# An xLSTM block with a look-up FFN on one core: two phases instead of one, the look-up spread over later blocks

## The reference

```
out = x + attn(xn) + ffn(xn)

attn(x): h = rmsnorm(x) * norm1
         q, k = h @ wq, h @ wk (8 heads of 32);  v, o = h @ wv, h @ w_og (8 heads of 64)
         i, f = 15 * tanh((h @ w_ig + b) / 15), 15 * tanh((h @ w_fg + b) / 15)
         F = cumsum(log_sigmoid(f));  D[s,t] = F[s] - F[t] + i[t], causal;  m = rowmax(D)
         C = (q @ k.T / sqrt(32)) * exp(D - m);  n = max(|rowsum(C)|, exp(-m))
         hh = rmsnorm_per_head((C / n) @ v) * mh_w * sigmoid(o)
         x1 = x + hh @ w_out
         return x1 + (silu(h2 @ w_gate) * (h2 @ w_up)) @ w_down,  h2 = rmsnorm(x1) * norm2   # 2048 wide

ffn(x):  gate, up, down = lut[gate_idx], lut[up_idx], lut[down_idx]    # 16 values, 1376 wide
         return (silu(x @ gate.T) * (x @ up.T)) @ down.T
```

## Time and profile before

| | |
|---|---|
| runs | 2776.36, 2777.57, 2778.02 us; median 2777.57 |
| profiled execution | 2779.31 us, its span 2777.5 us, mean granted clock 0.953 |
| TensorE, DVE, ScalarE, GpSimd busy | 2493.6, 1295.4, 809.4, 598.7 us |
| DMA | 431.78 MB, 155 GB/s over the span |

### The profile page before, as it was taken

The page is one execution under the profiler, slowest core; times in us unless marked ns, Lnnn a source line. Parts: engine busy times, 40 slices in busy tenths (PEclk is TensorE's granted clock), DMA queues, the critical chain, the costliest instruction groups (busy, mean ns, idle before and its releaser), DMA issues.

```text
span 2777.5 us, 32515 instructions
## 1 busy us (share of the span) xinstructions
PE 2493.6 (90%) x11024; PEld 2000.8 (72%) x11024; DVE 1295.4 (47%) x2240; ACT 809.4 (29%) x1474; POOL 598.7 (22%) x497
## 2 busy tenths in 40 slices
PE   4545877677999999999999999999999999999988
PEld 3324656566777788778877788778877888778877
DVE  6886874776134632364125622364235523463221
ACT  4653535552114211321123211321123211321111
POOL 1332540322111211131112211121112211121111
PEclk8757999889999999999999999999999999999999
DMA  5213765335542354244542355135533455135544
GB/s 198 72 46 122 283 235 197 129 122 224 193 173 92 137 189 182 83 141 167 200 153 91 129 197 197 72 134 188 184 128 107 152 189 196 62 138 188 194 182 154
DMA packets 95754, 431.78 MB, mean 155 GB/s; under 512 B 10496, under 2 KB 10496, under 8 KB 65664
## 3 DMA queue, kind: packets, MB, share of 16 engines
q1 hardware_dynamic: 80400, 393.56, 39.3%
q10 hardware_dynamic: 10464, 19.14, 2.1%
q0 software_dynamic: 4752, 17.30, 1.6%
HBM read 371.77 MB, written 58.20 MB: 155 GB/s over the span
## 4 chain that ended last, share of the span: by engine, by line
issue 52%; PE 16%; POOL 9%; ACT 3%; DVE 2%; DMA 2%; POOLq 0%; ACTq 0%; DVEq 0%; SPq 0%
POOL hidden_lo L1757 5%; PE acc L549 4%; PE up_bank L549 3%; PE gate_bank L549 3%; PE bank_b L549 3%; PE bank_a L549 2%; ACT look_w L924 1%; POOL MX L1770 1%; POOL vw L1785 1%; DMA gu<-gu_parts 1%; POOL rh L1702 1%; POOL rs L1702 1%; DMA first_rows<-xn 1%; DVE look_w L1281 0%; PE gate_bank L583 0%
## 5 line engine op out<-in xcount | busy, mean ns | idle before, releaser
L1757 POOL TENSOR_TENSOR hidden_lo<-hm,hidden_hi 128x512 fp32r<-128x512 f32 x216 | 279.6, 1294 | 1504.8 <-ACT hidden_hi L866 1504.7
L549 PE MATMUL acc<-dn,hidden_hi 128*128 128x512 f32 x1728 | 548.0, 399 | 24.6 <-POOL hidden_lo L1757 24.6
L1325 DVE SCALAR_TENSOR_TENSOR th<-th,gate_bank 128x512 f32<-128x512 f32 x216 | 147.8, 684 | 642.6 <-ACT th L861 642.6
L549 PEld LDWEIGHTS acc<-dn,hidden_hi 128*128 128x128 f32 x1728 | 324.0, 191 | 93.1 <-issue 20.2
L866 ACT ACTIVATE hidden_hi<-hm 128x512 fp32r<-128x512 f32 x216 | 135.9, 629 | 848.0 <-PE acc L549 824.2
L549 PE MATMUL gate_bank<-hT_hi,gu 128*128 128x512 f32 x1024 | 340.9, 394 | 30.4 <-DVE hT_lo L1547 19.4
L549 PE MATMUL up_bank<-hT_hi,gu 128*128 128x512 f32 x1024 | 339.7, 393 | 0.7 <-DVE hm L1331 0.6
L549 PE MATMUL acc<-dn,hidden_lo 128*128 128x512 f32 x864 | 339.6, 393 | 0.0
L861 ACT ACTIVATE th<-gate_bank 128x512 f32<-128x512 f32 x216 | 128.8, 596 | 471.8 <-PE gate_bank L549 471.8
L1331 DVE SCALAR_TENSOR_TENSOR hm<-th,up_bank 128x512 f32<-128x512 f32 x216 | 148.0, 685 | 241.6 <-PE up_bank L549 241.0
L549 PE MATMUL up_bank<-xT_hi,gu 128*128 128x512 f32 x704 | 256.8, 426 | 0.0
(11 more groups left out here) (233 smaller groups left out, 3711.3 us busy)
## 6 DMA issues: line engine op xcount, KB each, us to landing
gu<-gu_parts SPq DMA_DIRECT2D x200, 1024.0 KB, 4.8
dn<-dn_parts SPq DMA_DIRECT2D x200, 512.0 KB, 3.4
gu_parts<-gu SPq DMA_DIRECT2D x16, 1024.0 KB, 6.3
gu_parts<-look_w POOLq DMA_DIRECT2D x17, 512.0 KB, 3.1
ix<-idx ACTq DMA_DIRECT2D x33, 256.0 KB, 2.7
raw_gu<-w_gu SPq DMA_DIRECT2D x16, 512.0 KB, 6.9
qkT<-x SPq DMA_DIRECT2D x8, 1024.0 KB, 6.1
xn<-x SPq DMA_DIRECT2D x8, 1024.0 KB, 7.9
```

Source lines behind the costliest of these rows:

```text
L549: mm = pe.matmul(dst, l[a], r[c], start=first and k == 0 and n == 0, stop=last and k == len(lhs) - 1 and n == 2)
L1325: dve.scalar_tensor_tensor(th[:], th[:], 1.0, GB[:], ALU.add, ALU.mult).then_inc(vec_gate.sem, 1)
L1757: pool.tensor_tensor(HH[1][:], hm[:], HH[0][:].bitcast(f32), ALU.subtract).then_inc(pool_hid.sem, 1)
```

## The change

The work is put in another order, in two phases.

- Block 0: front, then units alone. Beside them the MLP weights of tiles 0 to 10 are split (`mlp_hi_`, `mlp_lo_`: gate, up and now also down on ScalarE and GpSimd) and stored; tiles 11 to 15 follow in block 1's front.
- MLP phase. For blocks 1 to 7: front, then 16 MLP tiles of the block before (`tiles(at)`, `mb = previous(at)`) with this block's units, out projection and h2 between tiles 0 to 10. x of the next block is normed at tiles 11 to 13. At the end the sums are copied to `XN[half]` and stored by SyncE as `mlp_rows`; x1 is stored as `x1_rows` at tile 11. Then 16 MLP tiles of block 7 without units (`TAIL`).
- Look-up: blocks 2 to 7 only, 11 chunks of gate, up or down per batch item, 5 in its first half and 6 in the second. DVE takes its steps by `TAKEN`: 6 or 8 at tile 8, and 11 or 13 at each of tiles 11 to 14. ScalarE takes at tile t those levels that the steps of tile t - 1 allow; levels of the first chunk at tile 0. Stores are now SyncE's. The buffers lie over the v and o weights, 4 MB, which SyncE loads again at the end of each of these blocks (`reload_vo`), behind the last chunks' stores.
- Ghost phase: for each block, 11 ghost tiles and nothing else of TensorE but the transposes of x, which is loaded, normed and transposed a second time. x, x1 and the MLP's rows are loaded (`rest`, 3 MB) and added at tile 3. SyncE stores the rows when the last sum is made.

The diff, cut to its core:

```diff
-NCH = 3 * NF
-PHASES = [0, 4, 21, 24, NCH]
+NCH = NF
+CHUNKS = [(0, 5), (5, NF)]
+TAKEN = [[0] * 8 + [6, 0, 0, 11, 11, 11, 11, 0], [0] * 8 + [8, 0, 0, 13, 13, 13, 13, 0]]
...
+# SyncE, one block of the MLP phase
+            def tiles(at):
+                b, half = at
+                mb = previous(at)
+                for t in range(NM):
+                    if t + 1 < NM:
+                        load_gu(MLP, mb, t + 1)
...
+                    else:
+                        load_gu(MLP, at, 0)
+                    load_dn(MLP, mb, t)
...
+                    if looks(at):
+                        ready = steps_taken(half, t - 1) // STEPS_V if t else 0
+                        for n in range(CHUNKS[half][0] + stored, ready):
+                            store_chunk(at, n)
+                            stored += 1
+                        if t == NM - 1:
+                            for n in range(*CHUNKS[half]):
+                                if n >= CHUNKS[half][1] - 2:
+                                    pair_stored(sp, at, n)
+                            reload_vo(1)
+                            reload_vo(2)
+                wait(sp, vec_out, mb, NB - 1)
+                first = (b * HALVES + half) * TOK + -TOK
+                sp.dma_start(rows_of(mlp_rows, first), XN[half][:]).then_inc(st_mlp[half], 16)
...
+# SyncE, the ghost phase
+                    for t in range(NF):
+                        if t + 1 < NF:
+                            load_gu(GHO, at, t + 1)
+                        else:
+                            load_gu(GHO, (b, half + 1), 0)
+                        load_dn(GHO, at, t)
+                        if t == 0:
+                            wait(sp, pe_xT, (b, half - 2), NB - 1)
+                            load_next(at)
+                            first = (b * HALVES + half) * TOK + -BATCH * SEQ
+                            sp.wait_ge(st_out[half], b * 16 + (16 - BATCH * 16))
+                            sp.dma_start(rest[half], rows_of(x, first)).then_inc(ld_rest[0], 16)
+                            sp.wait_ge(vec_rest.sem, vec_rest.before(at))
+                            sp.dma_start(rest[2], rows_of(x1_rows, first)).then_inc(ld_rest[1], 16)
+                            sp.dma_start(rest[3], rows_of(mlp_rows, first)).then_inc(ld_rest[2], 16)
+                    wait(sp, vec_out, at, NB - 1)
+                    sp.dma_start(rows_of(out, first), rest[half]).then_inc(st_out[half], 16)
...
+# ScalarE, tile t of the MLP phase, behind hid(t - 1) and tanh(t)
+                    if looks(at):
+                        ready = steps_of_levels(at[1], steps_taken(at[1], t - 1) if t else 0)
+                        look_up(at, min(ready, looked + 13) if t < NM - 2 else CHUNKS[at[1]][1] * STEPS_A)
+                        if t == NM - 2:
+                            upper(at, CHUNKS[at[1]][1] - 1)
...
+# DVE, tile t, behind gated(t) and product(t)
+                    if looks(at):
+                        look_up(at, steps_taken(half, t))
+                    if t == 11:
+                        ln_stats(at, XN[1 - half], 1 - half, b * 16 + (16 + 16 * half))
...
+                    for i in range(NB):
+                        x_T(at, i)
+                wait(dve, MLP.down, mb, NM - 1)
...
+                for i in range(NB):
+                    dve.tensor_copy(XN[half][:, i, :], ACC[i][:]).then_inc(vec_out.sem, 1)
...
+# TensorE, the ghost phase
+                    for t in range(NF):
+                        gate(GHO, at, t, act)
+                        up(GHO, at, t, act)
+                        if t >= NF - NB:
+                            x_T(at, t - NF + NB, XN[1 - half], ghosts=True)
+                        if t:
+                            down(GHO, at, t - 1, NF - 1)
+                    down(GHO, at, NF - 1, NF - 1)
```

More of the change, by code:

```diff
@@ L32, with steps_taken, steps_of_levels @@
 READ_BY = {upper: 3 + s for s, (lower, upper, bit) in enumerate(MUX)}
[L35 to L68, removed]
+TAKEN = [[0] * 8 + [6, 0, 0, 11, 11, 11, 11, 0], [0] * 8 + [8, 0, 0, 13, 13, 13, 13, 0]]
+def steps_taken(half, t):
+    return CHUNKS[half][0] * STEPS_V + sum(TAKEN[half][:t + 1])
+def steps_of_levels(half, j):
+    first, end = CHUNKS[half]
+    a = first * STEPS_A
     while a < end * STEPS_A:
         n, q = divmod(a, STEPS_A)
-        if q == 7:
+        if n == first:
+            need = 0
+        elif q == 7:
             need = n * STEPS_V
         elif q == 0:
-            need = n * STEPS_V if n in PHASES else (n - 1) * STEPS_V + 3
+            need = (n - 1) * STEPS_V + 3
         else:
@@ new lines, in up, with down @@
+            def up(of, at, t, act, stage=None):
+                z = slot(of, at, t)
+                if t == 0 and stage:
+                    wait(pe, vec_rows, stage, 0, "factors")
+                else:
+                    wait(pe, of.hm, at, t - 1)
+                split(UB[:], [(WGU[:, z, 1, 0, toks(k)], WGU[:, z, 1, 1, toks(k)]) for k in range(KT)],
+                      [pair(act, S_, k, S_) for k in range(KT)]).then_inc(of.up.sem, 1)
+            def down(of, at, t, last):
+                z = slot(of, at, t)
+                if t == 0:
+                    pe.wait_ge(vec_out.sem, vec_out.before(at))
+                pe.wait_ge(ld_dn[z], loads(of, at, t))
+                wait(pe, of.low, at, t, "lo")
@@ L838, in _ @@
-            for t in range(NF):
-                gate(LAST, t, t % 2, XT, loads(LAST, t))
-                up(LAST, t, t % 2, XT)
-                if t:
-                    if t == 1:
-                        pe.wait_ge(vec_out.sem, vec_out.before(LAST))
-                    down(LAST, t - 1, (t - 1) % 2, loads(LAST, t - 1), first=t == 1)
-            down(LAST, NF - 1, (NF - 1) % 2, loads(LAST, NF - 1), last=True)
+                    front((b, half))
+                    tiles((b, half))
+            tiles(TAIL)
@@ L1333, in front @@
             def front(at):
                 b, half = at
-                first, second = here(at, FIRST), here(at, SECOND) and PHASES[2] < NCH
+                first = here(at, FIRST)
                 R1 = r1[half]
```

1172 lines of the change are left out of this document (518 added, 654 removed).

## The result

The changed kernel takes **2904.05 us** (median of four runs, 2903.31 to 2906.26) against 2777.41 us before: a ratio of 1.046, 95% interval 1.044 to 1.048. The forecast was 2887 us, slower, with a range of 2750 to 2955. The profiled execution has a span of 2901.5 us.

A forecast was written before the change was run, and what follows sets the result against it. TensorE's order of work was taken to bound the kernel from block 2 on, look-up on DVE and ScalarE before. 2618 + 155 look-up + 100 ghost loads + 5 fronts + 9 tiles without units = 2887 us, range 2750 to 2955.

The forecast's parts named there:

- Start: Block 1's front was to begin at 192 us and its first gate tile at 245 us (220 to 275).
- 8.8 us a round: In block 0, each of eleven rounds of units beside an MLP tile's weight split takes 8.8 us, ending at 172 us.
- 13 beyond 40: Block 1's front: 40 us of groups and products, 53 with five splits, the last store and first stored-tile load.
- The bare blocks: A block without its 11 ghost tiles takes 217 us; block 1 needs 177 after its front's 40.
- Look-up: In blocks 2 to 7, look-up beside tiles adds 155 us in all, 4.7 us a chunk.
- ScalarE's 13 us round: In tiles 11 to 14, ScalarE needs 13 us a round against 8.16, with a 5.1 us store wait in it.
- Ghost phase: Eight blocks of 94.0 us, each 12.5 us late as gate(1) and gate(2) wait for weights: 100 us of lateness.
- Tiles without units: The 16 tiles without units take 133 us, plus 9 us for a late gu(1) and a slow gate.
- A: Whole kernel: ghost loads are never late and look-up costs 2 us a chunk, 2693 us; chance 0.15.
- B: Look-up beside tiles costs what it cost in block 1, 6.9 us a chunk: 2960 us; chance 0.15.
- C: Only the ghost phase is spared its lateness: 2787 us, or 2765 with the start at 223; chance 0.15.
- D: At the start, the DMA-bound weight split takes 12 us a round, start at 290 us: 2932 us; chance 0.08.

The follow-up runs named there:

- run 8: Changed kernel with a second buffer for the raw down weights of MLP tiles 1, 3, 5, 7 and 9: 2905.62 us, ratio 1.044.
- run 11: run 10 with two buffers for the raw down weights up to tile 15: 2673.86 us, ratio 0.961.
- run 1: Changed kernel without the look-up's steps and index loads, its stores and reloads kept: 2758.69 us, ratio 0.993.
- run 4: Changed kernel with stores sending other bytes, so ScalarE's look-up doesn't wait for them: 2891.16 us, ratio 1.041.
- run 3: Changed kernel with look-up steps spread, in unit tiles between unit_2 and unit_3: 2769.21 us; its second fence shows three tiles of the changed kernel.
- run 7: Changed kernel with ghost rows stored from ScalarE's queue and row loads spread over tiles 1 to 4: 2811.09 us, ratio 1.011.
- edits 3, 5 and 6: On the changed kernel: look-up steps in the middle of unit tiles, ghost rows stored from ScalarE's queue, row loads over tiles 1 to 4; together 2669.55 us.
- run 9: Changed kernel with mid-unit look-up steps, ghost rows stored from ScalarE's queue and row loads spread over tiles 1 to 4: 2669.55 us, ratio 0.961.
- runs 5 to 7: Changed kernel with ghost rows stored from ScalarE's queue (2838.99 us), with row loads spread over tiles 1 to 4 (2858.92 us), and with both (2811.09 us).
- run 10: run 9 with mlp_rows stored from ScalarE's queue too: 2681.14 us, ratio 0.964.
- run 5: Changed kernel with the ghost phase's row store moved from SyncE's to ScalarE's queue: 2838.99 us, ratio 1.022.

## Why the prediction held, step by step

The sum was closer than its terms. The front took 10 us more than its term, the six blocks with look-up 13 less, and these two errors nearly cancel, which is luck; the 14.5 us between 2887 and 2901.5 are about what the ghost phase took more (16.6).

**Start.** Right in place by luck, off in size, and with one cause misread. Block 1's front starts at 192.71 us, forecast 192; but I had 8.8 us a round and 20 us behind the last one. The eleven rounds took 10.6 us on average (run 8: the units' chain, not the weights), some 20 us more in all, and about as much less was left behind them: the last split starts at 178.5 us, only 14 before the front. The front took 62.8 us, not 53:

```profile
220.71 0.66 PE L596 MATMUL gate_bank<-ident,vw 128*128 128x128 f32 x2 [7.01 <-ACT qkT L967]
240.83 0.50 PE L561 MATMUL bank_b<-vo_w_hi,act_hi 128*128 128x512 f32 x1 [3.10 <-ACT th L984]
255.47 0.76 PE L561 MATMUL gate_bank<-act_hi,gu 128*128 128x512 f32 x1 [7.32 <-DMA gu<-mlp_parts]
```

I had counted ScalarE's five splits and the last store; not that three of the splits stand at the load of its raw down weights (6.7, 5.4 and 3.0 us, ScalarE's timeline), with qkT and the output gate's tanh behind it. With two buffers the front took 54.2 us (run 11). The sum's term "13 beyond 40" should have been 23.

**The bare blocks.** Right. Without look-up a block takes 215 to 219 us (forecast 217; the two of 219 with the loop's turn in them), block 1's rest 176.4 (177).

**Look-up.** Right in size: 149 us, 4.5 a chunk (forecast 155 and 4.7); 21 to 24 us in blocks with five chunks and 27 to 28.5 with six, fronts compared with run 1's. Wrong in which engine. I made ScalarE's 13 us round the worse bound, with the store wait of the earlier trace rows in it; taking that wait away gave 13 of 149 us (run 4). The 2 us a block for tiles 0, 8 and 9 weren't there either: these tiles take what they take in run 1, and all of the 149 us is in tiles 12 to 15. DVE, busy for 37.7 of the 42.8 us of three such tiles (run 3's second fence), was the bound as far as busy times tell, and its price per chunk was mis-sized. Its groups over the whole span (count, busy us, mean ns of one):

```profile
L1244 DVE COPY_PREDICATED look_w<-look_w 128x512 f32<-128x512 int32 x231 | 196.4, 887 | 23.6 <-ACT look_w L923 8.2 <-DVE look_w L1244 4.9 <-DVE look_w L1222 0.3
L1222 DVE TENSOR_SCALAR look_w<-raw_gu 128x512 int32<-128x512 int32 x99 | 45.3, 510 | 0.9
L1234 DVE TENSOR_SCALAR look_w<-raw_gu 128x512 int32<-128x512 int32 x33 | 13.9, 420 | 11.8 <-DMA raw_gu<-idx 11.8
```

That is 255.6 / 33 = 7.7 us a chunk where the earlier trace rows gave 6.5. Nearly all of the difference is GpSimd. Two copies and the GpSimd operation nearest to each:

```profile
869.79 0.73 DVE L1244 COPY_PREDICATED look_w<-look_w 128x512 f32<-128x512 int32 x1
870.41 1.29 POOL L1643 TENSOR_TENSOR look_w<-look_w 128x512 fp32r<-128x512 f32 x1 [6.13 <-ACT look_w L928]
882.07 1.57 POOL L1643 TENSOR_TENSOR look_w<-look_w 128x512 fp32r<-128x512 f32 x1 [3.04 <-ACT look_w L928]
882.85 1.38 DVE L1244 COPY_PREDICATED look_w<-look_w 128x512 f32<-128x512 int32 x1 [0.28 <-ACT look_w L923]
```

The copy that starts first takes its 0.73 us; the one that starts while GpSimd works ends 0.6 us after GpSimd does. Of the 231 copies in the span 45 start while a GpSimd operation runs: they take 1.57 us (median) and end 0.61 us behind it; the others take 0.75. That is some 32 us, 1.0 a chunk; the masks, slowed in the same way, add 0.3. The rows that the prediction took its 6.5 from had no such copy among them; the page of the kernel before, with 798 ns on average for the same copies, has some. The Trainium skill, "SBUF — State Buffer", section "SBUF: two separate sides", has it as a lock on a port pair that the two engines share, held for a whole instruction by whichever starts first (of VectorE's operations, by those with two inputs in SBUF, against a GpSimd operation that reads SBUF, and by those in a two-port mode). By that rule, the trace agrees. So ScalarE was put too slow and DVE too fast, and the size of this term came out right by luck.

**Ghost phase.** The mechanism was right, and the two late gates are where it put them to within 0.4 us; what each costs was less so. TensorE in the second ghost block (it starts at 2133.06 us), then SyncE's issues:

```profile
2143.95 0.79 PE L561 MATMUL gate_bank<-act_hi,gu 128*128 128x512 f32 x1 [5.29 <-DMA gu<-ghost_parts]
2158.51 0.49 PE L561 MATMUL gate_bank<-act_hi,gu 128*128 128x512 f32 x1 [3.48 <-DMA gu<-ghost_parts]
```

```profile
2135.86 0.41 SPq L544 DMA_DIRECT2D result<-look_w  x1
2136.38 0.44 SPq L432 DMA_DIRECT2D gu<-ghost_parts  x1
2144.45 2.36 SPq L432 DMA_DIRECT2D gu<-ghost_parts  x1
```

gu(1) is issued 3.3 us into the block (forecast 3.3) and used at 10.9 (11.1); gate(2) starts at 25.45 (25.1). The Trainium skill, "DMA: Bandwidth & Descriptors", section "Anatomy of one DMA", gives the 2.0 us and 436 GB/s that the prediction weighed. By that rule it would have started some 2 us sooner, an estimate from that page; the measurement decides for the row. A block takes 109.1 us, not 106.5. Compared with run 7's 95.8, the lateness is 13.3 us (forecast 12.5): spreading the rows takes 6.6 off (4.5 forecast), the store's move on top of that another 6.7 (8). The rest is that the block without lateness takes 95.8 and not 94.0: the last down group runs at a lower clock and takes 1.5 us more in three of eight blocks of the changed kernel, and in seven of eight of run 7. In the changed kernel the clock was 0.62 in one block where it was 1.00 in another:

```profile
2237.80:2242.30 4.50, 4.40 (x12) 3.48 (x13) 0.00 (x0) 0.00 (x0) 0.05 (x1) 0.62 0.03 7
2130.10:2133.00 2.90, 2.83 (x12) 2.33 (x13) 0.00 (x0) 0.00 (x0) 0.02 (x1) 1.00 0.00 0
```

Both stand behind the same 2.12 us wait for hidden_lo. Why the clock fell in one and not in the other stays open.

**Tiles without units.** 143.0 us, forecast 142.

**The rivals.** A (the cover holds) was wrong for this order of work, but it is what edits 3, 5 and 6 brought about: its 2693 us is close to run 9's 2670. B's 6.9 us a chunk (4.5 measured) and D's 12 us a round (10.6) weren't seen. C fell with the ghost blocks 109.1 us apart; runs 5 to 7 show that the store in front of the loads is one half of what they are late by and the row loads the other.

## What to carry to other kernels

Before moving side work beside a bound engine, add up the helper engine's work tile by tile, not block by block, and find the place in its queue where it waits for the bound engine anyway: the same steps cost 145 us in a heap, 127 spread but in front of the unit's mask, and 10 with two or three in each unit's own wait (medians of those runs less run 1's; between the last two place and number both changed). In a DMA queue a store that waits for results must not stand in front of loads that could go; but taking it out lets the loads go ahead of it, so look at who waits for the store. Read each large transfer as time for all behind it, and spread it. Where an engine idles and the waits name nothing, look at the DMA queues' instruction packets too.

## What the runs showed of the hardware

- A store on ScalarE's queue can land last although it is issued long before SyncE's loads are done. In run 10 the 1 MB store goes out at 1097.55 us, when SyncE's queue has 2.4 MB still to move. The queues' packets and MB in 1097.5 to 1101.3 us, then in 1101.3 to 1105.1 us (q1 is SyncE's, q10 ScalarE's):

```profile
q1 hardware_dynamic: 202, 1.51, 101.8%
q10 hardware_dynamic: 2, 0.00, 0.3%
```

```profile
q1 hardware_dynamic: 192, 0.85, 67.7%
q10 hardware_dynamic: 221, 0.45, 30.5%
```

  For 3.8 us the store moves nothing; the last store of the same run, issued with nothing else under way, has its first packet 0.92 us after the issue and lands after 4.3 us. Then the two queues move about as many packets each, but the store's are of 2 KB and the loads' of 4 and 8 KB, so that the loads get two thirds of the bytes. The store lands after 11.3 us, behind all the loads. The Trainium skill, "DMA: Bandwidth & Descriptors", section "Queues, rings and completion order", says that each DMA engine takes turns between queues packet by packet. By that rule the trace agrees in the second stretch, counted in the profile's packets; it doesn't explain the 3.8 us ahead of it.
- In run 5 the result's store took 11.0 us beside the row loads on ScalarE's queue, and in the changed kernel 5.3 us ahead of them in SyncE's own (medians of the DMA issues).
- TensorE can idle for 2 to 5 us at a loop's turn when 4 MB of loads have just been issued, with no wait that the profile names; in the kernel before, whose turns have no such burst, it is 1.0 us. The same 4 MB ahead of a front that isn't at a turn (block 3's in run 1) leave no idle time. Each time a 16 KB instruction packet starts 2.4 to 4.4 us before TensorE goes on (runs 5 and 7).
